# TensorE's steps regrouped and reordered in a software-pipelined audio tower (one Trainium2 core)

## What is computed

```python
# tokenizer: windows of 8 times, softmax over the window, weighted sum
h = sum_k x * softmax_k(x . w + b)                     # (128, 94, 64)
# attention on the normalised tokens, 8 heads
xn = layernorm(h)
h = h + sum_h softmax(xn Q_h K_h^T xn^T / 8) xn VO_h
# 4 causal heads x 4 experts of width 16, gates, two small layers, head gates
sx = layernorm(h) @ hl_w + hl_b
att = softmax(4 * (sx wq) (sx wk)^T + causal);  out = att @ (sx wv)
mixed = sum_e out_e * softmax_e(out . gate_w + gate_b)
f = layernorm(mixed + resid)
g = layernorm(relu(f fc1) fc2 + f)
h = h + g * softmax(g . fgate_w)
```

## Time and profile before

| | us |
|---|---|
| median of 3 runs (1027.72 to 1029.93) | 1029.25 |
| the profiled execution | 1028.16 |
| its span, first to last instruction | 1026.4 |
| PE busy / DVE busy / POOL busy / ACT busy | 928.4 / 855.5 / 770.6 / 742.0 |

### The profile page before, as it was taken

One profiled execution on the slowest core, in us unless ns is written; L12 is line 12 of the kernel. 1 busy time (PEld: TensorE's weight loads), 2 busy tenths in 40 slices (PEclk: granted clock), 3 DMA queues, 4 the chain that ended last, 5 costly groups with the idle time before them and its releaser, 6 DMA issues.

```text
span 1026.4 us, 39079 instructions
## 1 busy us (share of the span) xinstructions
PE 928.4 (90%) x16312; PEld 608.0 (59%) x16312; DVE 855.5 (83%) x1867; ACT 742.0 (72%) x2295; POOL 770.6 (75%) x1152
## 2 busy tenths in 40 slices
PE   3688999999999999999999999999999999989710
PEld 3255566666676666666666666666666666656510
DVE  3445688899989999899999998999989999997742
ACT  0345788788878888788878887888878788876400
POOL 2331335489887888789878888788878888988896
PEclk9679899999999999999999999999999999999955
DMA  6201111011111111111011111111100000001000
GB/s 191 71 1 39 39 39 40 10 38 36 42 42 44 44 43 44 44 43 38 19 37 40 43 43 44 44 44 43 43 14 13 7 10 13 13 14 23 7 8 11
...
## 3 DMA queue, kind: packets, MB, share of 16 engines
...
...
## 4 chain that ended last, share of the span: by engine, by line
PE 58%; DVE 31%; POOL 6%; ACT 2%; issue 1%; DMA 1%; SPq 0%; POOLq 0%; DVEq 0%; ACTq 0%
DVE pu L1445 8%; DVE mx L1442 7%; PE psum L685 7%; PE psum L695 7%; PE psum L774 7%; PE psum L703 4%; PE psum L723 4%; PE psum L800 3%; PE psum L789 3%; PE psum L606 3%; PE psum L627 3%; PE psum L619 3%; DVE ct L1453 2%; PE psum L677 2%; DVE xt L1358 2%; PE psum L759 2%
## 5 line engine op out<-in xcount | busy, mean ns | idle before, releaser
L1131 ACT ACTIVATE pu<-psum,mx 128x94 f32<-128x94 f32 x512 | 165.3, 357 | 15.6 <-DVE mx L1407 15.5
L1181 ACT ACTIVATE pT<-psum 96x512 f32<-96x512 f32 (+1 forms) x224 | 131.9, 603 | 53.0 <-PE psum L774 53.0
L464 POOL TENSOR_TENSOR pu<-pu,pr 128x752 f32<-128x752 f32 x96 | 137.4, 1445 | 21.0 <-DVE pr L1417 21.0
L501 POOL TENSOR_TENSOR st<-st,neg_half 128x12 f32<-128x12 f32 x64 | 145.5, 2273 | 5.0
L774 PE MATMUL psum<-ident_w,pu 128*96 128x128 f32 (+1 forms) x896 | 136.1, 282 | 1.4 <-ACT pu L1175 0.4
L774 PEld LDWEIGHTS psum<-ident_w,pu 128*96 128x96 f32 (+1 forms) x896 | 96.5, 135 | 55.3 <-issue 48.8
L1407 DVE TENSOR_REDUCE mx<-psum 128x8 f32<-128x752 f32 x96 | 89.9, 938 | 40.1 <-PE psum L685 39.9
L1445 DVE TENSOR_TENSOR pu<-psum,mx 128x1536 f32<-128x1536 f32 (+2 forms) x96 | 117.5, 1224 | 3.3
L1442 DVE TENSOR_REDUCE mx<-psum 128x16 f32<-128x1536 f32 (+2 forms) x96 | 115.0, 1198 | 3.5 <-PE psum L759 3.4
L800 PEld LDWEIGHTS psum<-gx,ct 128*128 128x128 f32 x768 | 92.9, 191 | 40.6 <-issue 34.1
L1131 ACT ACTIVATION_READ_ACCUMULATOR pu<-psum,mx 128x1 f32 x512 | 115.3, 225 | 0.0
...
## 6 DMA issues: line engine op xcount, KB each, us to landing
...
out_h<-ho SPq DMA_DIRECT2D x128, 16.0 KB, 1.4
out_h<-ho SPq DMA_DIRECT2D x128, 7.5 KB, 1.4
...
gx<-in_L_ffn_gate_w SPq DMA_DIRECT2D x16, 0.2 KB
fc<-in_L_ffn_fc_w SPq DMA_DIRECT2D x12, 1.0 KB
fc<-in_L_ffn_fc_b SPq DMA_DIRECT2D x12, 0.1 KB
```

The costliest lines, as they stand in the source:

```text
L464: pool.tensor_tensor(p, p, bcast(pr[:, j, :, :].rearrange("p a b -> p (a b)"), 2, NTOK), ALU.mult).then_inc(at_normed, 1)
L501: pool.tensor_tensor(st[:, k, 3, :], st[:, k, 2, :], neg_half[:, 0:NJ * NH], ALU.pow).then_inc(rstd, 1)
L1131: ins = act.activation(pu[:, j, par, hp, 0:NTOK], psum[:, (low, high)[par], NTOK * hp:NTOK * hp + NTOK], ACT.Exp, bias=mx[:, j, par, hp:hp ...
L1181: act.activation(pT3[j][:, f - (0, 4, 6)[i], :, :, :].rearrange("p e b t -> p (e b t)"), psum[0:rows, bank, :], ACT.Copy).then_inc(p_copie ...
```

## The change

All five engines' loop bodies are rewritten; the steps themselves, their instructions and their data are the same (SP 511, POOL 1148, PE 9120, ACT 1782 and VectorE 1867 instructions in both programs). What differs:

- TensorE's 36 steps of a turn stand in another order and in 19 groups. All waits of a group stand in front of its first step, and the others of the group have none. In a plain turn the order and the groups are: {`turn_p3(4)`, `mix3(0)`} {`mix3(1)`} {`score3(1)`} {`turn_rest`, `project(0)`, `turn_c(0)`} {`turn_p3(1)`, `layer1`} {`score3(2)`, `turn_c(1)`, `turn(0)`} {`front_turn`} {`turn(1)`, `project(1)`} {`turn_p3(0)`, `front_pair(1)`, `front_pair(0)`} {`turn_p3(3)`, `pool_x`} {`mix`} {`turn(2)`, `layer2`, `front_last`} {`score(0)`, `turn_p3(6)`} {`score(1)`, `give_outT`} {`score(2)`} {`mix3(2)`} {`give_out`, `score3(0)`} {`turn_p3(2)`, `turn_p3(5)`} {`turn_x`, `turn_c(2)`}. In a tok turn `tok_turn` stands in front of `front_last`, and `tok_score` of the next four quads behind `score(2)`.
- The banks differ for most steps.
- The orders on VectorE, GpSimd, ScalarE and SyncE follow, with other distances (the g - n of a step). The number of turns is the same apart from the labels: every engine's loop starts at q = -2 instead of -1 and its turns are counted differently.

The diff, cut to the steps and the waits that are spoken of (only added lines, de-indented):

```diff
@@ -388,17 +388,17 @@
...
+  if exists(g - 7, NQUAD):
+      sp.wait_ge(ho_made, 3 * g - 18)
+      store(g - 7, (v + 1) % 2)
+  if exists(g + 4, 26):
+      sp.wait_ge(x_filled, 3 * g + 15)
+      load(g + 4 + 6)
+  if exists(g, NQUAD):
+      sp.wait_ge(f_vc, g + 1)
+      move_v(v % 2)
+            for q in range(-2, 11):
...
@@ -535,65 +535,66 @@
...
+      norm_affine(g - 5, 0, fx_made, "j h", fx[:, :, 0:96].rearrange("p h (j c) -> p j h c", c=32))
...
+      scale(1, z_mul)
...
+      power3(g - 1)
...
+      gate_weight(g - 4)
...
+      norm_p(2)
...
+      norm_affine(g - 6, 1, fo_made, "h j", fo[:, v % 2, :].rearrange("p (j h c) -> p h j c", j=NJ, h=2))
...
+      norm_p(1)
...
+      gate_mul(v % 2)
...
+      head_mul(v % 2)
...
+      finish(g - 7, (v + 1) % 2, (g - 7) // 2)
...
+      norm_square(0, y_sq)
...
+      gate_scale((v + 1) % 2)
...
+      residual()
...
+      norm_power(g - 4, 0, y_rstd)
...
+      norm_square(1, z_sq)
...
+      ln_apply(g + 2, (v + 2) % 4)
...
+      scale(0, y_mul)
...
+      norm_power(g - 5, 1, z_rstd)
...
@@ -817,277 +818,293 @@
...
+      turn_p3(4, 7)
...
+      make_w(1)
...
+      mix3(v % 2, 0, 0)
...
+      mix3(v % 2, 1, 6, 7)
...
+      pe.wait_ge(s_shifted0, 2 * g - 8)
+      score3((v + 1) % 2, 1, 1)
...
+      pe.wait_ge(fx_made, 2 * g - 14)
...
+          pe.wait_ge(c_guarded, 3 * g - 15)
...
+      pe.wait_ge(at_xT, g - 1)
...
+          pe.wait_ge(g_ready, 1)
...
+          pe.wait_ge(c_guarded, 3 * g - 15)
...
+          pe.wait_ge(c_copied, 3 * g - 17)
...
+      turn_rest(fx[:, :, :], 6, r1_fxt)
...
+      project(v % 2, 0, 7, 5)
...
+      make_w2(6)
...
+      turn_c(0, 0)
...
+          pe.wait_ge(c_guarded, 3 * g - 15)
...
+      turn_p3(1, 7)
...
+      layer1(6)
...
+          pe.wait_ge(c_copied, 3 * g - 17)
...
+      turn_c(1, 1)
...
+      turn(g - 1, 0, 0)
...
+      front_turn(7)
...
+          pe.wait_ge(g_ready, 1)
...
+      turn(g - 1, 1, 2)
...
+      project(v % 2, 1, 3, 4)
...
+          pe.wait_ge(c_guarded, 3 * g - 15)
...
+          pe.wait_ge(at_xT, g - 1)
...
+      turn_p3(0, 6)
...
+      front_pair(1, 5, 1)
+      front_pair(0, 0, 7)
...
+      front_resid(4)
...
+      make_g(4)
...
+          pe.wait_ge(x_scaled, 3 * g)
...
+      pe.wait_ge(x_scaled, 3 * g)
...
+          pe.wait_ge(at_xT, g - 1)
...
+      turn_p3(3, 2)
...
+      pool_x(g - 1, 6)
...
+      mix((v + 1) % 4, (0, 4, 5, 7))
...
+          pe.wait_ge(x_scaled, 3 * g)
...
+      turn(g, 2, 1)
...
+      layer2(3)
...
+      tok_turn(5)
...
+      front_last(2, 6)
...
+      score(v % 2, 0, 3, 4)
...
+      score(v % 2, 1, 0, 1)
...
+      give_outT(7)
...
+      tok_score(g + 1, 2)
...
+      mix3((v + 1) % 2, 2, 0)
...
+          pe.wait_ge(at_maxed1, 2 * g - 2)
...
+          pe.wait_ge(tok_shifted, ((g + 1) // 4) + 1)
...
+          pe.wait_ge(at_exped, 3 * g - 5)
...
+      turn_p3(2, 7)
+      turn_p3(5, 0)
...
+      turn_x((v + 3) % 4, 6)
...
+      turn_c(2, 5)
...
@@ -1201,127 +1218,128 @@
...
+      front_kp(v % 2, 1, 5)
...
+      front_sxT(v % 2, 0)
+      front_kp(v % 2, 0, 7)
...
+      copy_p3(3, 2)
...
+      copy_k(v % 2, 2, 3)
...
+      front_res(4)
...
+      front_kp(v % 2, 2, 1)
...
+      store_h(g + 3, 6)
...
+      exp3(2)
...
+      copy_cT(2, 5)
+      copy_cT(1, 4)
...
+      copy_cT(0, 0)
+      copy_cT(3, 7)
...
+      front_vc(v % 2, 6)
+      front_kp(v % 2, 3, 2)
...
+      copy_p3(6, 5)
...
+      copy_p3(2, 7)
...
+      copy_p3(5, 0)
...
+      copy_xT((v + 1) % 2, 6)
...
+      copy_p3(4, 7)
...
+      exp_all(1)
...
+      copy_c((v + 1) % 2, 2, 5)
...
+      copy_fxT(6)
...
+      copy_k((v + 1) % 2, 0, 7)
+      copy_k((v + 1) % 2, 1, 5)
...
+      copy_c((v + 1) % 2, 0, 0)
...
+      apply3(g + 1)
...
+      copy_p3(1, 7)
...
+      hidden(6)
...
+      copy_c((v + 1) % 2, 1, 1)
...
+      front_xT(7)
...
+      exp3(1)
...
+      copy_k((v + 1) % 2, 3, 4)
...
+      copy_p3(0, 6)
...
@@ -1509,58 +1527,16 @@
...
+      variance(0, y_eps)
...
+      scale_x(g - 1, 2, 1)
...
@@ -1569,39 +1545,44 @@
...
+      least(g - 3, 1, 0, 1)
...
+      least(g - 3, 2, 5, 6)
...
+      sums(g - 3, 0)
...
+      head_shift(g - 10)
...
+      split_w()
...
+      soft_tok(g, 2)
...
+      guard(v % 2, 2, 0)
...
+      add_out(g - 4, 7)
...
+      guard(v % 2, 0, 0)
...
+      guard(v % 2, 1, 6, 7)
...
@@ -1609,10 +1590,54 @@
...
+      head_sum(g - 10)
...
+      sums(g - 3, 1)
...
+      soft(g - 5, 2, 2)
...
+      scale_x(g - 1, 0, 0)
...
+      turn_p(0)
...
+      scale_x(g - 1, 1, 2)
...
+      turn_p(2)
...
+      mask_hidden()
...
+      turn_p(1)
...
+      sums_inv(v % 2)
...
+      norm_tok(g)
...
+      mix_experts(g - 7)
...
+      head_reduce()
...
+      ln_stats(g - 1)
...
+      dve.wait_ge(r1_fc2, g - 7)
+      mask_second(3)
+            for q in range(-2, 11):
...
```

718 lines of the change are left out of this document (299 added, 419 removed).

## The result

| | before | after |
|---|---|---|
| median of 6 runs each, us | 1028.74 (1027.72 to 1029.93) | 1025.01 (1023.06 to 1025.48) |
| profiled execution / its span | 1028.16 / 1026.4 | 1025.48 / 1023.7 |
| plain turn / tok turn, in the middle | 27.17 / 31.11 | 27.50 / 30.88 |

The ratio of after to before is 0.9959, with a 95% interval of 0.9946 to 0.9972: 0.4% faster. Over all rounds of this study single executions of the kernel before took 1025.2 to 1034.1 us (medians 1027.9 to 1028.7), the longer ones mostly with a lower mean granted clock of TensorE (0.954 in those of 1026 us, 0.946 in those of 1030.5), so a difference of one or two us between two single traces says little. Lines have moved: on TensorE one further than in before (`turn_rest` is L806, `project` L678), on ScalarE 17 and on VectorE 18 further (`guard` is L1471).

A forecast was written before the change was run, and what follows sets the result against it. TensorE bounds the middle turns, chains the fill, GpSimd the drain. Plain turn: 27.17 - 0.33 - 0.27 + 0.6 = 27.17; tok turns gain 2.4 us in all, ends 0: 1028.16 - 2.4 = 1025.8 profiled, 1026.9 us median; range 1013 to 1036 (own 1021 to 1033).

The forecast's parts named there:

- A met wait costs nothing, a change of size the same with or without it: Between TensorE's steps: met waits are free, tile-size changes cost 0.09 us on leaving, 0.05 to 0.10 on entering.
- The rival with prefetched weights: TensorE's unwaited size changes: weights load across them, saving 0.4 us per turn; 1014 us, 1000 at best; chance 15%.
- Removed work: Plain turn: 0.33 us less from fewer size changes on TensorE, 0.27 less from `pool_x` no longer waiting for `scale_x`.
- The wait that comes: `turn_rest` on TensorE waits for VectorE's last `guard`, 13.73 us against 13.12: 0.6 us late every plain turn.
- 0.07 for the two semaphores: Handovers at both ends of VectorE's run from `mask_second` to last guard: 0.07 us added to its 13.66.
- Parts of the same 0.6: `mix3(2)` about 0.3 us and `turn_x` about 0.45 late; TensorE's loss there isn't lost again at `turn_rest`.
- The tok turn: Tok turn falls from 31.11 to 30.9 us; 0.6 lost at `give_out` waiting for `soft_tok`, none at the next `turn_rest`.
- The ends: Fill and drain of the kernel: taken as 0 in sum, 4 us either way.
- `turn_x` behind `exp_s(2)`: Fill: `turn_x` now needs `exp_s(2)` of the same turn, costing about 1 us in two or three turns.
- once, 2 to 3 us: Fill: `front_turn` moves behind `project(0)` and `turn(0)`, removing TensorE's one-time stand for its chain, 2 to 3 us.
- The slow rival: VectorE's run grows at the `c_guarded` wait of `turn_rest`, each 0.1 us costing 3.2 us: 1036 us; chance 23%.
- a semaphore more: Slow rival's example of what could add to two more late waits, together 0.2 us in a turn.

The follow-up runs named there:

- ungroup: Changed kernel with the waits of eight groups on TensorE given back to their own steps; order and banks untouched: 1019.3 us.
- late_first: Changed kernel with the wait met last put first at `turn_rest`, `mix3(2)` and `turn_x`, and repeated waits of a group dropped: 1019.6 us.
- extra8: Changed kernel with eight more, long-met waits behind the late one at `turn_rest`, in 23 turns: 1027.1 us.
- run_short: Changed kernel with VectorE's `head_shift` moved in front of `mask_second` and `gate_sum` behind the guards: 1026.8 us.
- centre_later: Changed kernel with VectorE's `centre` behind `least(1)` instead of in front, and GpSimd's `norm_square(1)` behind `ln_apply`: 1026.4 us.
- both_short: Changed kernel with the edits of run_short and centre_later together: 1028.1 us.
- front_early: Changed kernel with `front_turn` of quad 0, once, ahead of `make_w`, `make_w2` and `project(0)`; ScalarE's `apply3` and `front_xT` ahead of `copy_m`: 1032.2 us.

## Why the prediction was right, and which steps of it were not

The forecast was 1026.9 us; measured were 1025.0, within the range and faster as the largest chance had it. That the number is so near is luck, two errors of opposite sign: the turns were to give 2.4 us and took 3.6 (from the second `give_out` to the last; about 5 while all steps exist), the ends were to give nothing and gave 6.3 (7.9 before the second `give_out`, less 1.6 behind the last).

**A met wait costs nothing, a change of size the same with or without it: right.** In after no wait stands in front of `project(0)` and `turn_c(0)` behind `turn_rest`: `project(0)` takes 547.61 to 548.45 = 0.84 us, as in before with its waits. Its weights load no earlier either, in before (first row) 0.01 us ahead of the first matmul, in after with it:

```profile
522.37 0.30 PEld L677 LDWEIGHTS psum<-xT,g_w 64*128 64x128 f32 x4 [0.17 <-issue]
```
```profile
547.61 0.30 PEld L678 LDWEIGHTS psum<-xT,g_w 64*128 64x128 f32 x4 [0.17 <-issue]
```

ungroup says it by experiment: eight steps with their waits back, and nothing slower. The rival with prefetched weights is out. The Trainium skill, page TensorEngine Tiling, section Key Properties, has TensorE drain at a change of mode; by that rule, the trace agrees. The Trainium skill's page TensorE: Matmul & The Clock Gate, section Step-by-step: what each phase is for, would let weights be pulled ahead to other rows or to the background buffer; over a change of size no run here shows it.

**Removed work: right.** 27.17 - 0.33 - 0.27 = 26.57 us was the turn without any lateness. The steps of after, added up between starts without their lateness, give 26.6. `pool_x` doesn't wait.

**The wait that comes: the right place, 0.6 us where 0.93 was measured** (27.50 - 26.57). The reason given for it, that the group's `project(0)` needs bank 7, is half of it: `turn_rest` needs bank 6, which the same `mix3(1)` fills, and waits for the guard without the group too (ungroup). The step that failed in the turns is "0.07 for the two semaphores". VectorE's run was put at 13.66 us; from `mask_second` at 560.79 to the end of the guards at 573.23 + 1.27 = 574.50 it is 13.71:

```profile
560.79 0.35 DVE L1510 SCALAR_TENSOR_TENSOR ft<-fx,psum 128x192 f32<-128x192 f32 x1 [0.71 <-PE psum L814]
...
573.23 1.27 DVE L1471 SCALAR_TENSOR_TENSOR ct<-sxT,psum 128x512 f32<-128x512 f32 x2
```

But the semaphores cost 0.04 + 0.26 = 0.30 us, since the wait for the guard is followed by four others in its list. late_first and extra8 show that term by itself, 0.2 us less and 0.16 more at that place. The remaining 0.1 is 0.05 of the run (in which `head_shift` alone takes 0.46 instead of the 0.28 put down) and 0.05 of TensorE's path.

**"Parts of the same 0.6": right as long as VectorE's run is unbroken, and wrong as soon as it is not.** In after the lateness at `mix3(2)` (0.41 us over its unhindered start) and at `turn_rest` (0.41 to 0.50) add up to that of one run. run_short, centre_later and both_short show that they are limits of their own: one shortened, the others hold.

**The tok turn: right in sum, 30.9 for 30.88,** but not in parts. `give_out` waits for `soft_tok` 0.24 us, 0.3 over its unhindered start, not 0.6, and `turn_rest`, which was to lose nothing, waits for its guard 0.43 us as in other turns (519.77 above). The 1.48 us of `soft_tok` were read from the earlier trace rows, where its middle instruction takes 0.78 us, as in every tok turn from 300 us on in before; in after it takes 0.23, and the step 0.94. Before, then after:

```profile
528.95 0.78 DVE L1335 TENSOR_SCALAR tok_mb<-tok_m,tokb 96x16 f32<-96x16 f32 x1
```
```profile
511.64 0.23 DVE L1353 TENSOR_SCALAR tok_mb<-tok_m,tokb 96x16 f32<-96x16 f32 x1
...
512.51 0.56 PE L713 MATMUL psum<-ident_w,oT 64*64 64x64 f32 x12 [0.24 <-DVE tok_e L1355]
```

Why the same instruction takes three times as long in one kernel stays open. The turn behind a tok turn, which was to lose 0.1 less, takes 27.50 us like the others.

**The ends: wrong.** "I take 0, and 4 us either way" fails in three terms. `turn_x` behind `exp_s(2)`, put at 1 us in two or three turns, does wait, 5.09, 1.15 and 0.36 us in the first turns that have it:

```profile
44.92 0.87 PE L672 MATMUL psum<-ident_w,xn 128*128 128x128 f32 x3 [5.09 <-ACT pu L1148]
```

But it costs nothing in sum: before has other waits in the same stretch (1.47 and 2.95 us), and both kernels are level at `score(2)`, 59.4 us. `give_out` of quad 0 is 2.4 us later for `tok_score`, whose move the forecast did not price. `front_turn` was put at "once, 2 to 3 us"; front_early measures 7.1, of which about 6 hold against before. What was missed is that the low clock comes on top of the idle stretch: the matmuls behind it run at half the clock (before: `make_w2` 6.9 us, `tok_score` 5.33; after: 5.1 and 3.69). The drain, put at nothing, took 1.6 us; no run looks into that.

**The slow rival** (VectorE's run grows, "a semaphore more") is what happened in the turns; its price of 3.2 us for each 0.1 us of turn counts all 32 turns and is about a third too high: 0.8 us in four turns, 0.2 in each, came to some 5 us in about 24 turns. That the total still went down is due to the fill alone.
